# A graph network's attention scores: fp32 products replaced by products of rounded parts and rests

## Chip, core and metric

The kernel runs on one core of a Trainium2 chip. The metric is the device time of one execution in microseconds (us). The engines are PE (TensorE; PEld is its weight load), DVE (VectorE), ACT (ScalarE), POOL (GpSimd) and SP (SyncE, here a queue that issues DMAs). A queue's own DMA issues are shown as SPq, ACTq and POOLq.

## What is computed

Two graph layers over 50,000 nodes and 25,000 edges sorted by destination. The first integrates a graph convolution by four Runge-Kutta steps, the second is an attention layer. Only the attention's first part is touched:

```python
q = (x @ Wq + bq).reshape(n, H, C)          # n nodes, H = 4 heads of C = 32
k = (x @ Wk + bk).reshape(n, H, C)
v = (x @ Wv + bv).reshape(n, H, C)
e = (edge_attr @ We).reshape(-1, H, C)      # edge_attr: 25000 x 32
kj = k[src] + e
vj = v[src] + e
alpha = jnp.einsum('ehc,ehc->eh', q[dst], kj) / np.sqrt(C)
```

Afterwards alpha goes through a softmax per destination and weighs the sum of vj.

## The kernel before

Edges lie in 196 tiles (TE) of 128. The program runs in stages with a barrier between them: `prepare`, `local_pass` (nodes without edges, 0 to about 3250 us of the span with `prepare`), the nine `coupled_stages` (to about 7556 us), and `attention` with `scores`, `shares_beside_far` and `finish_coupled`. This document is about `scores`, lines 1425 to 1569, from about 7563 to 8286 us.

`scores` runs over 98 pairs of edge tiles. Each engine has a list of steps with lags, which `skewed` turns into a loop: at turn t a step of lag n works on pair t - n. Buffers are rings of 4 or 2 slots; `s` is the pair's number modulo 4.

- POOL, `gather` (L1483): four indirect DMAs for each pair, which fetch the rows of x of both tiles' sources and destinations (128 rows of 512 bytes each) into `a_rows`. The pair four back must have been turned. The four issues of all 98 pairs are written out without a loop.
- PE, `turn` (L1502): four 128x128 transposes into one bank. PE, `multiply` (L1510), one pair later: for each of the two tiles, three matmuls that add into one bank of 384 columns (key, value, query): the edges' features with a row of ones against `w_edge` with a row of biases (L1518, 33 rows, 384 wide), the source rows against Wk and Wv (L1520, 256 wide), the destination rows against Wq (L1522, 128 wide). All are fp32, and an fp32 matmul shows as two MATMUL records.
- ACT, `copy` (L1530): the turned rows from PSUM to `a_xt`. ACT, `take` (L1536): value and scaled query out of the banks.
- DVE, `weigh` (L1555): query times key, reduced over each head. DVE, `keep` (L1566), two turns later: 8 columns of alpha.
- SP, `load` (L1464): one DMA of edge features for each pair (33 rows); `store` (L1470) writes the values.

Ahead of the loop SP issues 14 DMAs of weights and biases (`a_weights` 224), for which PE waits.

`local_pass` already works with rounded parts: `product` (L665) adds hi*hi, hi*lo and lo*hi in fp32r, an fp32 whose mantissa the writing engine rounds. There an fp32r matmul shows as one MATMUL record; the profile prints its type as f32. The hi part is written by an ACT copy (L930), the lo part by a DVE subtraction (L985).

Of the kernel before, what the change touches and what calls it, by code (L numbers as in the profile page):

```python
# [1398 lines left out]
def attention(nc, a, S, counts, m):  # L1399

    from contextlib import ExitStack
    ctx = ExitStack()

    def sb(name, shape, dt=F32):
        t = ctx.enter_context(nc.sbuf_tensor(name, list(shape), dt))
        m[name] = t
        return t

    with ctx:
        sb("alpha", [P, TE, HEADS])  # L1410
        sb("w_kvq", [P, 3 * D])
        sb("w_edge", [ED + 1, 3 * D])
        sb("w_skip", [P, D])
        sb("w_up", [P, D])
        sb("w_down", [P, D])
        sb("b_skip", [P, 1])
        sb("b_up", [P, 1])
        sb("b_down", [P, 1])
        sb("neg_half", [P, 2])
        scores(nc, a, S, counts, m)  # L1420
        shares_beside_far(nc, a, S, counts, m)
        finish_coupled(nc, S, counts, m)


def scores(nc, a, S, counts, m):
# [4 lines left out]
    def sb(name, shape, dt=F32):  # L1430
        return ctx.enter_context(nc.sbuf_tensor(name, list(shape), dt))

    pairs = TE // 2
    v, psum, ident = nc.vector, m["psum"], m["ident"]
    ph = counts.phase(pairs, {"gathered*": 64, "own_in*": 16, "turned": 1, "copied": 1,
                              "product": 1, "query": 1, "values": 1, "weighed": 1, "alpha": 1, "stored*": 16})

# [3 lines left out]
    with ctx:  # L1441
        rows = sb("a_rows", [P, 4, 4, D])
        edge = sb("a_edge", [ED + 1, 4, 2 * P])
        xt = sb("a_xt", [P, 2, 4 * P])
        query = sb("a_q", [P, 2, 2, D])
# [3 lines left out]
        with nc.Block() as block:  # L1449
            @block.sync  # L1450
            def _(sp):
                for n, key in enumerate(("Wk", "Wv", "Wq")):
                    sp.dma_start(m["w_kvq"][:, n * D:(n + 1) * D], a["L1_gnn_" + key]).then_inc(S["a_weights"], 16)
                for n in range(2):
                    sp.dma_start(m["w_edge"][0:ED, n * D:(n + 1) * D], a["L1_gnn_We"]).then_inc(S["a_weights"], 16)
                for n, key in enumerate(("bk", "bv", "bq")):
                    sp.dma_start(m["w_edge"][ED:ED + 1, n * D:(n + 1) * D], a["L1_gnn_" + key].unsqueeze(0)
                                 ).then_inc(S["a_weights"], 16)
# [5 lines left out]
                def load(j, s):  # L1464
                    if past(j, 4):
                        sp.wait_ge(S["product"], ph.at("product", j - 4))
                    sp.dma_start(edge[:, s, :], a["edge_attr"][:, bass.ds(j * (2 * P), 2 * P)]
                                 ).then_inc(S[f"own_in{s}"], 16)

# [5 lines left out]
                for s in range(4):  # L1475
                    sp.wait_ge(S[f"stored{s}"], ph.ring_end("stored", s))
                sp.wait_ge(S["a_weights"], 224)

# [19 lines left out]
            def _(pe):  # L1498
                pe.wait_ge(S["a_weights"], 224)
                pe.wait_ge(S["a_zeros"], 1)  # L1500

                def turn(j, s):  # L1502
                    pe.wait_ge(S[f"gathered{s}"], ph.ring_at("gathered", j, s))
                    if past(j, 2):
                        pe.wait_ge(S["copied"], ph.at("copied", j - 2))
                    for i in range(4):
# [3 lines left out]
                def multiply(j, s):  # L1510
                    pe.wait_ge(S["copied"], ph.at("copied", j))
                    pe.wait_ge(S[f"own_in{s}"], ph.ring_at("own_in", j, s))
                    if past(j, 2):
                        pe.wait_ge(S["values"], ph.at("values", j - 2))
                        pe.wait_ge(S["weighed"], ph.at("weighed", j - 2))
                    for i in range(2):
                        bank = psum[2 + 2 * (s % 2) + i]
                        nc.tensor.matmul(bank[:, 0:3 * D], edge[:, s, i * P:(i + 1) * P], m["w_edge"][:],  # L1518
                                         start=True, stop=False)
                        nc.tensor.matmul(bank[:, 0:2 * D], xt[:, s % 2, i * P:(i + 1) * P], m["w_kvq"][:, 0:2 * D],  # L1520
                                         start=False, stop=False)
                        last = nc.tensor.matmul(bank[:, 2 * D:3 * D], xt[:, s % 2, (2 + i) * P:(3 + i) * P],  # L1522
                                                m["w_kvq"][:, 2 * D:3 * D], start=False, stop=True)
                    last.then_inc(S["product"], 1)

                skewed(pe, pairs, [(0, turn), (1, multiply)])

            @block.scalar
            def _(act):
                def copy(j, s):  # L1530
                    act.wait_ge(S["turned"], ph.at("turned", j))
                    if past(j, 2):
                        act.wait_ge(S["product"], ph.at("product", j - 2))
                    nc.scalar.activation(xt[:, s % 2, :], psum[s % 2][:], ACT.Copy).then_inc(S["copied"], 1)

                def take(j, s):  # L1536
# [11 lines left out]
                    last.then_inc(S["query"], 1)  # L1548
                skewed(act, pairs, [(0, copy), (1, take)])

            @block.vector
            def _(dve):
                v.memset(m["w_edge"][0:ED, 2 * D:3 * D], 0.0).then_inc(S["a_zeros"], 1)

# [11 lines left out]
                def keep(j, s):  # L1566
                    dve.wait_ge(S["alpha"], ph.at("alpha", j))
                    v.tensor_copy(m["alpha"][:, bass.ds(j * 2, 2), :], al[:, s, :, :])
                skewed(dve, pairs, [(1, weigh), (3, keep)])

# [685 lines left out]
```

## Time and profile before

| | |
|---|---|
| median of 3 runs | 9125.33 us (9120.25 to 9130.2) |
| profiled execution | 9196.13 us, span 9194.4 us |
| PE busy | 6718.1 us, 73% |
| DVE busy | 6441.7 us, 70% |
| POOL busy | 5499.4 us, 60% |
| ACT busy | 3381.1 us, 37% |
| mean granted clock of PE | 0.862 |

Busy shares are means over very different stages. A stage that ends at a barrier is read by itself: which engine is never idle in it, and how long the others wait for that one. A matmul's duration reaches over its neighbours, since matmuls are pipelined; what one costs is the distance from its start to the next start. The granted clock is a share of 2.4 GHz: 0.50 is 1.2 GHz.

### The profile page before, as it was taken

What the parts mean: (1) busy time and instruction counts of PE and PEld (TensorE: products, weight loads), DVE (VectorE), ACT (ScalarE), POOL (GpSimd) and SP (SyncE); (2) the same over time, 40 slices, a digit from 0 to 9 for tenths busy, and PEclk for the clock granted to TensorE, in tenths of its full rate; (3) what the DMA queues carried; (4) which work ended last, traced back from release to release, by engine and by line L of the source; (5) the groups of instructions that cost most, each with busy time, mean ns of one, the idle gap of its engine ahead of it and who ended that gap; (6) DMA issues with size and microseconds to landing.
All of it is one profiled execution on the core that took longest, in us unless ns stands there. A gap on an engine that the chain in (4) does not pass through costs nothing. (4 is left out here: it accounts for less than half of the span.)

```text
span 9194.4 us, 168134 instructions
## 1 busy us (share of the span) xinstructions
PE 6718.1 (73%) x36044; PEld 5385.6 (59%) x36044; DVE 6441.7 (70%) x17476; ACT 3381.1 (37%) x9316; POOL 5499.4 (60%) x6135
## 2 busy tenths in 40 slices
PE   1600399889988966988897797789666669996665
PEld 0100388888888844766675576667444545554544
DVE  2910388677877888779778977987798981117976
ACT  0000366666666645641361164136100111113323
POOL 0067687777877756755575476557332655545667
PEclk9655799999999977999999999999888985557889
DMA  9333345765444455879879988988898762214544
GB/s 142 86 97 97 100 145 146 123 141 139 143 144 138 139 147 156 249 241 292 250 244 312 315 253 260 335 271 259 280 308 280 210 174 61 60 56 141 169 142 125
DMA packets 1968800, 1693.27 MB, mean 184 GB/s; under 512 B 183280, under 2 KB 1879809, under 8 KB 1968301
## 3 DMA queue, kind: packets, MB, share of 16 engines
q1 hardware_dynamic: 1541549, 1107.88, 42.2%
q0 software_dynamic: 160192, 335.62, 13.1%
q10 hardware_dynamic: 266560, 244.12, 7.8%
q8 instruction: 191, 3.13, 0.2%
q14 instruction: 308, 2.52, 0.1%
HBM read 1063.01 MB, written 624.28 MB: 184 GB/s over the span
## 5 line engine op out<-in xcount | busy, mean ns | idle before, releaser
L1193 PE MATMUL bank<-c_rows,c_sums 128*128 128x256 f32 (+1 forms) x3920 | 1336.0, 425 | 1032.3 <-DVE c_rows L1284 620.7
L680 PE MATMUL bank<-wf_w,c_xt 128*128 128x256 f32 x6272 | 1539.2, 390 | 3.7 <-DVE y L1358 2.6
L1193 PEld LDWEIGHTS bank<-c_rows,c_sums 128*128 128x128 f32 x3920 | 696.7, 203 | 1396.9 <-DVE c_rows L1284 699.3
L1225 ACT ACTIVATE c_xt<-bank 128x512 f32<-128x512 f32 (+1 forms) x980 | 563.5, 575 | 2424.2 <-PE bank L1203 1408.8
L1166 POOL DMA_INDIRECT c_rows<-t_tab,src_row x784 | 872.5, 1113 | 970.7 <-PE bank L1193 807.4
L680 PEld LDWEIGHTS bank<-wf_w,c_xt 128*128 128x128 f32 x6272 | 1231.7, 197 | 185.5 <-issue 3.6
L1284 DVE SCALAR_TENSOR_TENSOR c_rows<-bank,carry,c_rows 32x256 f32<-32x256 f32 (+1 forms) x1950 | 910.6, 467 | 495.6 <-issue 340.5
L1166 POOL DMA_INDIRECT c_rows<-z_tab,src_row x784 | 768.9, 981 | 304.7 <-issue 193.0
L985 DVE TENSOR_TENSOR lx_lo<-bank,lx_hi 128x512 fp32r<-128x512 f32 (+1 forms) x1000 | 658.1, 658 | 350.8 <-ACT lx_hi L930 284.5
L930 ACT ACTIVATE lx_hi<-bank 128x512 fp32r<-128x512 f32 (+1 forms) x1000 | 561.1, 567 | 577.4 <-PE bank L899 457.0
L564 POOL DMA_INDIRECT x_tab<-x_in,stage_pos x396 | 406.3, 1026 | 599.5 <-DMA x_in<-in_x 479.3
L670 PE MATMUL bank<-wf_hi,lx_hi 128*128 128x256 f32 x3200 | 711.2, 304 | 73.5 <-issue 56.4
L1309 DVE SCALAR_TENSOR_TENSOR c_u<-bank,lead,c_own 128x256 f32<-128x256 f32 x1764 | 759.5, 469 | 0.0
L1173 POOL TENSOR_TENSOR c_inv<-c_ss,c_neg_half 128x2 f32<-128x2 f32 x588 | 419.0, 713 | 420.5 <-DVE c_ss L1380 174.0
L670 PE MATMUL bank<-wf_lo,lx_hi 128*128 128x256 f32 x3200 | 643.4, 282 | 0.7 <-issue 0.7
L670 PE MATMUL bank<-wf_hi,lx_lo 128*128 128x256 f32 x3200 | 642.1, 282 | 1.5 <-issue 1.5
L1239 ACT ACTIVATE c_squares<-y,c_root_deg 128x256 f32<-128x256 f32 x980 | 489.9, 500 | 393.5 <-ACT y L1231 238.9
L1203 PE MATMUL bank<-ident,c_u 128*128 128x128 f32 x3724 | 591.5, 281 | 1.0 <-DVE c_u L1309 0.9
L670 PEld LDWEIGHTS bank<-wf_hi,lx_hi 128*128 128x128 f32 x3200 | 494.8, 192 | 106.0 <-issue 84.0
L1203 PEld LDWEIGHTS bank<-ident,c_u 128*128 128x128 f32 x3724 | 487.0, 146 | 97.8 <-issue 6.5
L670 PEld LDWEIGHTS bank<-wf_lo,lx_hi 128*128 128x128 f32 x3200 | 497.3, 191 | 1.4 <-issue 1.4
L670 PEld LDWEIGHTS bank<-wf_hi,lx_lo 128*128 128x128 f32 x3200 | 496.0, 191 | 2.3 <-issue 2.3
(295 smaller groups left out, 15231.3 us busy)
## 6 DMA issues: line engine op xcount, KB each, us to landing
c_z<-z_tab SPq DMA_DIRECT2D x882, 256.0 KB
c_sums<-sum_tab SPq DMA_DIRECT2D x980, 128.0 KB
z_tab<-lz SPq DMA_DIRECT2D x400, 256.0 KB
t_tab<-lt SPq DMA_DIRECT2D x400, 256.0 KB
z_tab<-y ACTq DMA_DIRECT2D x392, 256.0 KB
c_own<-z_tab SPq DMA_DIRECT2D x392, 256.0 KB
t_tab<-y ACTq DMA_DIRECT2D x392, 256.0 KB
c_own<-t_tab SPq DMA_DIRECT2D x392, 256.0 KB
```

Source lines behind the costliest of these rows:

```text
L670: last = nc.tensor.matmul(out, x(k), w[:, k, :], start=(n == 0), stop=(n == 3 * ks - 1 and not bias))
L680: last = nc.tensor.matmul(out, x(k), w[:, k, :], start=(k == 0), stop=(k == ks - 1))
L930: nc.scalar.activation(x_hi[:, k].rearrange("p k n -> p (k n)")[:, 0:n], psum[k][:, 0:n], ACT.Copy).then_inc(S["high"], 1)
L985: v.tensor_tensor(x_lo[:, k].rearrange("p k n -> p (k n)")[:, 0:n], psum[k][:, 0:n], x_hi[:, k].rearrange("p k n -> p (k n)")[:, 0:n].bitc ...
L1166: pool.indirect_dma_start(out=rows[:, s, i, 0:XW] if first else rows[:, s, i, :], out_offset=None, in_=source, in_offset=bass.IndirectOffs ...
L1173: nc.gpsimd.tensor_tensor(inv[:, s, :], ss[:, s, :], m["c_neg_half"][:], ALU.pow).then_inc(S["inverted"], 1)
L1193: nc.tensor.matmul(psum[s % 2][:, i * win:(i + 1) * win], sums[:, s, i, :], rows[:, s, i, 0:win], start=True, stop=True).then_inc(S["summe ...
L1203: last = nc.tensor.transpose(psum[2 + s % 2][:, k * H2 + i * P:k * H2 + (i + 1) * P], u[:, s % 2, i, k * P:(k + 1) * P], ident[:])
L1225: nc.scalar.activation(xt[:, s % 2].rearrange("p k n -> p (k n)")[:, 0:n], psum[2 + s % 2][:, 0:n], ACT.Copy).then_inc(S["copied"], 1)
L1239: last = nc.scalar.activation(m["c_squares"][:, i, :], y[:, s, i, :], ACT.Square, scale=m["c_root_deg"][:, bass.ds(j * 2 + i, 1)], accum_o ...
L1284: v.scalar_tensor_tensor(rows[p0:p0 + 32, s, i, 0:win], before, m["carry"][p0:p0 + 32, bass.ds(j * 2 + i, 1)], rows[p0:p0 + 32, s, i, 0:wi ...
L1309: last = v.scalar_tensor_tensor(u[:, s % 2, i, 0:win], psum[s % 2][:, i * win:(i + 1) * win], m["lead"][:, bass.ds(j * 2 + i, 1)], u[:, s ...
```

## The change

Every fp32 product of `scores` becomes products of fp32r parts. `a_xt` becomes `x_hi` (an ACT copy that rounds) and `x_lo` (a DVE subtraction, new step `low`, from PSUM and `x_hi`). Each of L1520 and L1522 becomes three matmuls: x_hi w_hi, x_hi w_lo, x_lo w_hi. The edges' product becomes one fp32r matmul of 98 rows. The stationary side holds edge features rounded, their rests, and the features rounded again (32 rows each), then two rows of ones; the moving side holds the rounded weights twice, the weights' rests, and the bias' rounded part and rest. For that SP loads the edge features three times (96 rows), ACT rounds all 96 rows (`edge_high`, 96x256), and DVE subtracts in the middle 32 rows (`edge_low`, 32x256). The weights are split once at the start: two ACT copies of 384 columns and four DVE instructions, two of which wait for the one ahead, behind the 18 weight DMAs (`a_weights` 288), with small masks ahead of them. PE waits for all of it (`a_split` 5). `turn` now waits for `low` of two pairs back, `multiply` for `low` and `edge_low` of its pair, `load` for `edge_low` of four pairs back.

The diff, with most of its context left out:

```diff
@@ -1409,7 +1409,6 @@
...
         sb("w_kvq", [P, 3 * D])
-        sb("w_edge", [ED + 1, 3 * D])
         sb("w_skip", [P, D])
...
@@ -1432,16 +1431,30 @@
...
     v, psum, ident = nc.vector, m["psum"], m["ident"]
-    ph = counts.phase(pairs, {"gathered*": 64, "own_in*": 16, "turned": 1, "copied": 1,
-                              "product": 1, "query": 1, "values": 1, "weighed": 1, "alpha": 1, "stored*": 16})
+    ph = counts.phase(pairs, {"gathered*": 64, "own_in*": 48, "turned": 1, "copied": 1,
+                              "product": 1, "query": 1, "values": 1, "weighed": 1, "alpha": 1, "stored*": 16,
+                              "low": 1, "edge_high": 1, "edge_low": 1})
...
         rows = sb("a_rows", [P, 4, 4, D])
-        edge = sb("a_edge", [ED + 1, 4, 2 * P])
-        xt = sb("a_xt", [P, 2, 4 * P])
+        K = 3 * ED + 2
+        edge = sb("a_edge", [3 * ED, 4, 2 * P])
+        edge_parts = sb("a_edge_parts", [K, 4, 2 * P], F32R)
+        w_edge = sb("a_w_edge", [K, 3 * D])
+        w_edge_most = sb("a_w_edge_most", [K, 3 * D])
+        w_edge_hi = sb("a_w_edge_hi", [K, 3 * D], F32R)
+        w_edge_lo = sb("a_w_edge_lo", [K, 3 * D])
+        w_edge_parts = sb("a_w_edge_parts", [K, 3 * D], F32R)
+        w_hi = sb("a_w_hi", [P, 3 * D], F32R)
+        w_lo = sb("a_w_lo", [P, 3 * D], F32R)
+        is_rest = sb("a_is_rest", [P, 1])
+        not_rest = sb("a_not_rest", [P, 1])
+        x_hi = sb("a_x_hi", [P, 2, 4 * P], F32R)
+        x_lo = sb("a_x_lo", [P, 2, 4 * P], F32R)
         query = sb("a_q", [P, 2, 2, D])
...
@@ -1451,10 +1464,13 @@
...
                     sp.dma_start(m["w_kvq"][:, n * D:(n + 1) * D], a["L1_gnn_" + key]).then_inc(S["a_weights"], 16)
+                sp.wait_ge(S["a_zeros"], 1)
                 for n in range(2):
-                    sp.dma_start(m["w_edge"][0:ED, n * D:(n + 1) * D], a["L1_gnn_We"]).then_inc(S["a_weights"], 16)
+                    for part in range(3):
+                        sp.dma_start(w_edge[part * ED:(part + 1) * ED, n * D:(n + 1) * D], a["L1_gnn_We"]
+                                     ).then_inc(S["a_weights"], 16)
                 for n, key in enumerate(("bk", "bv", "bq")):
-                    sp.dma_start(m["w_edge"][ED:ED + 1, n * D:(n + 1) * D], a["L1_gnn_" + key].unsqueeze(0)
+                    sp.dma_start(w_edge[3 * ED:K, n * D:(n + 1) * D], a["L1_gnn_" + key].partition_broadcast(2)
                                  ).then_inc(S["a_weights"], 16)
...
@@ -1463,9 +1479,10 @@
...
                     if past(j, 4):
-                        sp.wait_ge(S["product"], ph.at("product", j - 4))
-                    sp.dma_start(edge[:, s, :], a["edge_attr"][:, bass.ds(j * (2 * P), 2 * P)]
-                                 ).then_inc(S[f"own_in{s}"], 16)
+                        sp.wait_ge(S["edge_low"], ph.at("edge_low", j - 4))
+                    for part in range(3):
+                        sp.dma_start(edge[part * ED:(part + 1) * ED, s, :],
+                                     a["edge_attr"][0:ED, bass.ds(j * (2 * P), 2 * P)]).then_inc(S[f"own_in{s}"], 16)
...
@@ -1474,7 +1491,7 @@
...
                     sp.wait_ge(S[f"stored{s}"], ph.ring_end("stored", s))
-                sp.wait_ge(S["a_weights"], 224)
+                sp.wait_ge(S["a_weights"], 288)
...
@@ -1496,33 +1513,33 @@
...
             def _(pe):
-                pe.wait_ge(S["a_weights"], 224)
-                pe.wait_ge(S["a_zeros"], 1)
+                pe.wait_ge(S["a_split"], 5)
...
                     if past(j, 2):
-                        pe.wait_ge(S["copied"], ph.at("copied", j - 2))
+                        pe.wait_ge(S["low"], ph.at("low", j - 2))
                     for i in range(4):
...
                 def multiply(j, s):
-                    pe.wait_ge(S["copied"], ph.at("copied", j))
-                    pe.wait_ge(S[f"own_in{s}"], ph.ring_at("own_in", j, s))
+                    pe.wait_ge(S["low"], ph.at("low", j))
+                    pe.wait_ge(S["edge_low"], ph.at("edge_low", j))
                     if past(j, 2):
...
                         bank = psum[2 + 2 * (s % 2) + i]
-                        nc.tensor.matmul(bank[:, 0:3 * D], edge[:, s, i * P:(i + 1) * P], m["w_edge"][:],
+                        nc.tensor.matmul(bank[:, 0:3 * D], edge_parts[:, s, i * P:(i + 1) * P], w_edge_parts[:],
                                          start=True, stop=False)
-                        nc.tensor.matmul(bank[:, 0:2 * D], xt[:, s % 2, i * P:(i + 1) * P], m["w_kvq"][:, 0:2 * D],
-                                         start=False, stop=False)
-                        last = nc.tensor.matmul(bank[:, 2 * D:3 * D], xt[:, s % 2, (2 + i) * P:(3 + i) * P],
-                                                m["w_kvq"][:, 2 * D:3 * D], start=False, stop=True)
+                        for x, w in ((x_hi, w_hi), (x_hi, w_lo), (x_lo, w_hi)):
+                            nc.tensor.matmul(bank[:, 0:2 * D], x[:, s % 2, i * P:(i + 1) * P], w[:, 0:2 * D],
+                                             start=False, stop=False)
+                        for n, (x, w) in enumerate(((x_hi, w_hi), (x_hi, w_lo), (x_lo, w_hi))):
+                            last = nc.tensor.matmul(bank[:, 2 * D:3 * D], x[:, s % 2, (2 + i) * P:(3 + i) * P],
+                                                    w[:, 2 * D:3 * D], start=False, stop=(n == 2))
                     last.then_inc(S["product"], 1)
                 skewed(pe, pairs, [(0, turn), (1, multiply)])
...
@@ -1531,7 +1548,13 @@
...
                         act.wait_ge(S["product"], ph.at("product", j - 2))
-                    nc.scalar.activation(xt[:, s % 2, :], psum[s % 2][:], ACT.Copy).then_inc(S["copied"], 1)
+                    nc.scalar.activation(x_hi[:, s % 2, :], psum[s % 2][:], ACT.Copy).then_inc(S["copied"], 1)
+                def edge_high(j, s):
+                    act.wait_ge(S[f"own_in{s}"], ph.ring_at("own_in", j, s))
+                    if past(j, 4):
+                        act.wait_ge(S["product"], ph.at("product", j - 4))
+                    nc.scalar.activation(edge_parts[0:3 * ED, s, :], edge[:, s, :], ACT.Copy).then_inc(S["edge_high"], 1)
...
@@ -1546,11 +1569,44 @@
...
                     last.then_inc(S["query"], 1)
-                skewed(act, pairs, [(0, copy), (1, take)])
+                act.wait_ge(S["a_weights"], 288)
+                nc.scalar.activation(w_hi[:], m["w_kvq"][:], ACT.Copy).then_inc(S["a_high"], 1)
+                nc.scalar.activation(w_edge_hi[:], w_edge[:], ACT.Copy).then_inc(S["a_high"], 1)
+                skewed(act, pairs, [(0, edge_high), (0, copy), (1, take)])
...
             def _(dve):
-                v.memset(m["w_edge"][0:ED, 2 * D:3 * D], 0.0).then_inc(S["a_zeros"], 1)
+                v.memset(w_edge[0:3 * ED, 2 * D:3 * D], 0.0).then_inc(S["a_zeros"], 1)
+                v.tensor_reduce(is_rest[:], ident[:, 2 * ED:3 * ED], AX.X, ALU.add).then_inc(S["a_split"], 1)
+                dve.wait_ge(S["a_split"], 1)
+                v.tensor_tensor(is_rest[:], is_rest[:], ident[:, K - 1:K], ALU.add).then_inc(S["a_split"], 1)
+                dve.wait_ge(S["a_split"], 2)
+                v.tensor_scalar(not_rest[:], is_rest[:], -1.0, 1.0, ALU.mult, ALU.add).then_inc(S["a_split"], 1)
+                for s in range(4):
+                    v.tensor_scalar(edge_parts[3 * ED:K, s, :].rearrange("p (i c) -> p i c", c=P),
+                                    ident[3 * ED:K, :].unsqueeze(1).to_broadcast([2, 2, P]), 0.0, 1.0,
+                                    ALU.mult, ALU.add)
+                dve.wait_ge(S["a_weights"], 288)
+                dve.wait_ge(S["a_high"], 2)
+                dve.wait_ge(S["a_split"], 3)
+                v.tensor_tensor(w_lo[:], m["w_kvq"][:], w_hi[:].bitcast(F32), ALU.subtract)
+                v.tensor_tensor(w_edge_lo[:], w_edge[:], w_edge_hi[:].bitcast(F32), ALU.subtract)
+                v.tensor_scalar(w_edge_most[:], w_edge_hi[:].bitcast(F32), not_rest[0:K, :], None, ALU.mult
+                                ).then_inc(S["a_split"], 1)
+                dve.wait_ge(S["a_split"], 4)
+                v.scalar_tensor_tensor(w_edge_parts[:], w_edge_lo[:], is_rest[0:K, :], w_edge_most[:], ALU.mult, ALU.add
+                                       ).then_inc(S["a_split"], 1)
+                def low(j, s):
+                    dve.wait_ge(S["copied"], ph.at("copied", j))
+                    v.tensor_tensor(x_lo[:, s % 2, :], psum[s % 2][:], x_hi[:, s % 2, :].bitcast(F32), ALU.subtract
+                                    ).then_inc(S["low"], 1)
+                def edge_low(j, s):
+                    dve.wait_ge(S["edge_high"], ph.at("edge_high", j))
+                    mid = edge_parts[ED:2 * ED, s, :]
+                    v.tensor_tensor(mid, edge[ED:2 * ED, s, :], mid.bitcast(F32), ALU.subtract
+                                    ).then_inc(S["edge_low"], 1)
...
@@ -1566,7 +1622,7 @@
...
                     v.tensor_copy(m["alpha"][:, bass.ds(j * 2, 2), :], al[:, s, :, :])
-                skewed(dve, pairs, [(1, weigh), (3, keep)])
+                skewed(dve, pairs, [(0, edge_low), (0, low), (1, weigh), (3, keep)])
...
```

## Rows read from the trace of the kernel before

**Rows 1.** The page: granted clock of TensorE, 40 slices of 230 us.

```profile
PEclk9655799999999977999999999999888985557889
```

**Rows 2.** Busy time of each engine in 100 us of the stage.

```profile
core 0: us, PE busy (x) PEld busy (x) DVE busy (x) ACT busy (x) POOL busy (x), PEclk, DMA share, GB/s
7800.00:7900.00 100.00, 100.00 (x225) 57.27 (x224) 15.11 (x56) 19.17 (x70) 52.65 (x56) 0.50 0.21 59
```

**Rows 3.** Groups of instructions in the stage: count, busy, mean ns, idle before.

```profile
L1518 PE MATMUL bank<-w_edge,a_edge 33*128 33x384 f32 x392 | 322.5, 925 | 7.0 <-issue 4.9 <-DVE a_w L1558 2.1
...
L1490 POOL DMA_INDIRECT a_rows<-x_tab,src_row x196 | 184.8, 943 | 254.5 <-PE bank L1507 215.9 <-issue 33.8 <-remote 4.5
...
L1534 ACT ACTIVATE a_xt<-bank 128x512 f32<-128x512 f32 x98 | 58.7, 599 | 36.4 <-issue 27.0 <-remote 7.6
```

**Rows 4.** Instructions in order of time, one period: start, duration, engine, idle before.

```profile
7905.04 1.06 PE L1507 MATMUL bank<-ident,a_rows 128*128 128x128 f32 x4
...
7906.03 1.65 PE L1518 MATMUL bank<-w_edge,a_edge 33*128 33x384 f32 x2
...
7906.37 0.94 POOL L1490 DMA_INDIRECT a_rows<-x_tab,src_row  x1 [2.48 <-PE bank L1507]
...
7907.60 1.22 PE L1520 MATMUL bank<-w_kvq,a_xt 128*128 128x256 f32 x2
7907.62 0.95 POOL L1490 DMA_INDIRECT a_rows<-x_tab,src_row  x1 [0.30 <-issue]
...
7908.62 0.63 PE L1522 MATMUL bank<-w_kvq,a_xt 128*128 128x128 f32 x2
...
7909.18 1.65 PE L1518 MATMUL bank<-w_edge,a_edge 33*128 33x384 f32 x2
...
7912.20 1.06 PE L1507 MATMUL bank<-ident,a_rows 128*128 128x128 f32 x4
```

**Rows 5.** The same view, the local pass: 256 wide at 1.2 GHz.

```profile
1048.19 0.41 PE L670 MATMUL bank<-w_hi,lx_hi 128*128 128x256 f32 x1
1048.41 0.41 PE L670 MATMUL bank<-w_lo,lx_hi 128*128 128x256 f32 x1
```

**Rows 6.** The same view, the local pass: 128 wide at 1.2 GHz.

```profile
3248.20 0.63 PE L670 MATMUL bank<-w_lo,lx_hi 128*128 128x128 f32 x2
3248.63 0.63 PE L670 MATMUL bank<-w_hi,lx_lo 128*128 128x128 f32 x2
```

**Rows 7.** The same view, the local pass: 256 wide at 2.4 GHz.

```profile
2001.20 0.39 PE L670 MATMUL bank<-wf_hi,lx_lo 128*128 128x256 f32 x2
2001.42 0.39 PE L670 MATMUL bank<-wf_hi,lx_hi 128*128 128x256 f32 x2
```

**Rows 8.** Groups of instructions of the local pass, 1500 to 3000 us.

```profile
L985 DVE TENSOR_TENSOR lx_lo<-bank,lx_hi 128x512 fp32r<-128x512 f32 x609 | 417.1, 685 | 239.3 <-ACT lx_hi L930 184.3 <-issue 53.4
...
L829 POOL DMA_INDIRECT lxo<-x_tab,own_row x135 | 138.8, 1028 | 37.5 <-issue 37.5
...
L1008 DVE TENSOR_TENSOR lrest<-lx_add,b 128x256 f32<-128x256 f32 x68 | 28.6, 420 | 0.0
```

**Rows 9.** Instructions in order of time: start of the stage.

```profile
7564.21 1.02 POOL L1490 DMA_INDIRECT a_rows<-x_tab,src_row  x1 [0.60 <-issue]
...
7568.04 0.94 POOL L1490 DMA_INDIRECT a_rows<-x_tab,dst_row  x1 [0.30 <-issue]
...
7568.98 0.43 SPq L1462 DMA_DIRECT2D b_down<-in_L_gnn_b  x1
...
7571.31 1.11 PE L1507 MATMUL bank<-ident,a_rows 128*128 128x128 f32 x4 [20.82 <-DMA a_rows<-x_tab,dst_row]
```

**Rows 10.** The same view: end of the stage and one copy after it.

```profile
8285.59 0.31 DVE L1568 COPY alpha<-a_al 128x8 f32<-128x8 f32 x3
...
8297.64 0.38 ACT L1831 ACTIVATE fl_xt<-bank 128x256 f32<-128x256 f32 x1
```

**Rows 11.** The gathers of the coupled stages: duration min/median/max in ns.

```profile
L1166 POOL DMA_INDIRECT c_rows<-t_tab,src_row x784: 940/979/1805, 4049.4 to 7067.2; - x196
```

## The prediction

> **What bounds it now.** Read the page's clock line first, then the busy times of the stage, its groups, and one period in order of time. In the page's line the clock falls to about half in slices 33 to 36 [rows 1], which is where `scores` lies. There PE is busy 100 of 100 us at a granted clock of 0.50, that is 1.2 GHz, while DVE is busy 15, ACT 19 and POOL 53 [rows 2]. PE has hardly any idle time ahead of its groups, and POOL's gathers wait 215.9 us in all for PE's transposes [rows 3]. So PE is the bound. One period from transposes to transposes is 7912.20 - 7905.04 = 7.16 us [rows 4]. It holds 7906.03 - 7905.04 = 0.99 of transposes, and for each tile 7909.18 - 7906.03 = 3.15, made of 1.57 for the edges' product, 1.02 for key and value, 0.56 for the query; 0.99 and twice 3.15 are 7.3, less what the last of a pair overlaps. 98 periods are 701 us of the stage, which takes 8285.9 - 7563.5 = 722 us [rows 9, 10].
>
> **PE after.** One MATMUL of rounded parts, 256 wide, costs 1048.41 - 1048.19 = 0.215 us at 1.2 GHz [rows 5]; two of 128 columns cost 3248.63 - 3248.20 = 0.43, so one costs 0.215 as well: half the width brings nothing [rows 6]. At 2.4 GHz two of 256 cost 0.22 [rows 7]. No row shows 384 columns nor 98 rows. The bounds are one 256-wide (0.215) and two (0.43); I take 1.5 times the 256-wide, 0.32, since from 128 to 256 the fixed part already vanished. A tile is then 0.32 + 3 x 0.215 + 3 x 0.215 = 1.61 against 3.15, although it goes from 6 MATMUL records to 7. A pair at 1.2 GHz is 0.99 + 2 x 1.61 = 4.2 us, 4.4 with the upper bound; at 2.4 GHz it is about half. So PE gives back 2.9 us of each 7.16 at the least.
>
> **What is late next.** POOL. Four gathers cost it 4 x (0.943 + 0.30) = 4.97 us [rows 3, 4]; start to start they are 7907.62 - 7906.37 = 1.25. In each period of before it waits 2.48 us for PE [rows 4], and 4.97 + 2.48 - 0.30 = 7.15 closes the period. With PE at 4.2, POOL never waits and the pair costs 4.98. Only 2.18 of PE's 2.9 us reach the end; the other 0.8 becomes PE idle time.
>
> **The added work, each beside that bound of 4.98.**
> - DVE: `low` is the local pass' own instruction at 0.685; `edge_low`, 32 rows by 256, is at most the 128x256 subtraction at 0.42 [rows 8]. With the 15.1 per 100 us of today, 1.08 a pair [rows 2], DVE has 2.2 of 4.98. If that cover were gone it would add up to 1.1 a pair, 108 us.
> - ACT: `edge_high`, 96x256, is near the 128x256 copy at 0.38 [rows 10]; 1.37 of today [rows 2] becomes 1.75. Its wait for features stands ahead of `copy` in ACT's order, so a late load would hold the transposed rows, `low`, and the next `turn`. Loads are issued when `edge_low` of four pairs back is done, some three periods or 15 us ahead.
> - SP: two more issues a pair at 0.43 each [rows 9]; with the first and the store that is 1.7 of 4.98. The wait for `edge_low` now stands ahead of the store of an older pair, which nobody awaits before four more pairs.
> - DMA: 96 rows of 1 KB for 33, while the DMA engines are 21% busy at 59 GB/s [rows 2]; hidden.
> - The hand-over from `turn` to `multiply`: 0.99, copy 0.60 [rows 3], `low` 0.69 and 0.27 for each of two hand-overs (a gather starts at 7906.37 on transposes that end at 7906.10 [rows 4]) make 2.8 us, in which PE multiplies the pair before for 3.2. At 2.4 GHz that is 1.7 us and PE may wait, but a pair is still under 4.98.
> - The start: four more DMA issues of 0.43 move the last weight by 1.7 us, then two ACT copies and four DVE instructions (up to 0.69 each) with hand-overs make 4 to 5. The first transposes, at 7571.3 today [rows 9], come at about 7578. POOL holds four pairs of slots, so it needs them only at 7564.2 + 4 x 4.98 = 7584.1. Price nothing to 6; I take 3, for the first turns of a loop, where the order of time of before has gaps.
>
> **The sum.** First gather at 7564.2 [rows 9]; 98 x 4.98 = 488.0 brings its last issue to 8052.2. A gather lands 7571.31 - 7568.98 = 2.3 later [rows 9]: 8054.5. Then come the last transposes, 0.99, two products of 3.2 (the pair before waits behind them in PE's order), and about 2 for taking (1.37 less the copy's 0.60) and weighing (1.08) [rows 2, 3]: 8063.9. With 3 for the start it is 8067. A gather may also be dearer beside a busier DVE: beside 609 of the same subtraction it took 1.028 with 0.278 between [rows 8], 0.063 more, or 25 us over 392 gathers; DVE is much less loaded here, so I take 8 of nothing to 25. The stage ends at 8075 and not at 8285.9: 211 us less. The other stages aren't touched. The profiled execution of 9196 us would be 8985. It is 71 us (0.8%) above the median of the runs, and no row says where these lie; I carry the difference over whole: 9125.3 - 211 = 8914 us.
>
> **Rivals.**
> 1. Port: `edge_low` reads two operands from SBUF, as no per-pair instruction of the stage does today. If each held up the gather beside it by its whole 0.42, a pair would cost 5.40: 41 us back, 8955. For it: a gather of the coupled stages has taken up to 1.805 against a minimum of 0.940 [rows 11]. Against it: the median there is 0.979. The Trainium skill, page "SBUF — State Buffer", section "Who interferes with whom", says that a DVE instruction with two SBUF inputs contends with a GpSimd instruction that reads SBUF, and that whichever came first holds the port for its whole duration. By it `edge_low` would be the only added per-pair instruction to contend, as `low` has one operand in PSUM. The rows neither confirm it nor exclude it.
> 2. No gain: the steps don't overlap, because a wait of `turn` or `multiply` serialises them. Then a pair is 0.99 + 0.60 + 0.69 + 3.2 + take 0.8 and four hand-overs of 0.27, 7.36 us against 7.16, and the time stays at 9125, 20 more at the most. Against it: two PSUM banks and two slots for each step, as before. A partial chain of 5.5 to 7 us would give 8965 to 9110.
> 3. Slower: gathers at 1.805 [rows 11] plus 0.30 are 8.4 a pair, +124 us, 9249. It decides from 7.16 / 4 = 1.79 us a gather. For it: POOL would run back to back for 490 us with rounding traffic beside it. Against it: even the local pass' mean was 1.31.
> 4. More gain: part of POOL's 0.30 between gathers may be the profiler's own, and PE may rise to 2.4 GHz. At 1.15 a gather, 0.093 less, it is 36 us more, and the tail 3 less: about 8875. No row separates that part; the profiled execution's 71 us above the median are what speaks for it.
>
> **Chances.** Forecast 0.70 (8890 to 8935); port 0.12 (8935 to 8965); more gain 0.07 (8850 to 8890); partial chain 0.04; no gain 0.03; slower 0.04. The range is 8878 to 8962: the forecast, the port and part of the larger gain, about 0.85. A measurement of this kernel can tell about 0.2%, 18 us, from no change. Faster is 0.93, same 0.03, slower 0.04.
>
> **What would show it.** Right: POOL nearly 100% busy or in its 0.30 gaps through the stage, gathers with no wait for PE, a pair every 4.98 us, PE idle some 0.8 us (more if its clock rises) waiting for a gather's landing, and the stage 490 to 515 us long. Three MATMULs 0.215 apart at 1.2 GHz in place of 1.02 show the parts' price; 0.32 from the edges' product to the next shows the 384 columns. Wrong: gathers whose mean is 1.0 or more while `edge_low` runs (rival 1); PE or DVE with waits for each other and POOL still waiting for PE (rival 2); an ACT wait for a load at `edge_high`; or a gap of tens of us before the first transposes.

## Result, and the profile after

| | before | after |
|---|---|---|
| median of 4 runs | 9127.76 us (9120.25 to 9134.89) | 8918.78 us (8910.9 to 8923.26) |
| profiled span | 9194.4 us | 8917.7 us |
| `scores`, first gather to the last copy of alpha | 721.7 us | 505.8 us |

The ratio is 0.977, with a 95% interval of 0.9753 to 0.9787: 209 us less (194 to 225), against a forecast of 211. The profiled spans differ by 277: 216 of it is the stage's, and 60 lies ahead of the stage, in code that the change leaves alone (the first gather of `scores` starts at 7504.3 where [rows 9] have 7564.2). In a later profile of the kernel before with one part of the stage left out (`before_half_gathers`, below) it starts at 7490.2. So the 71 us by which the profiled execution lay above the median came ahead of the stage.

The whole stage after, each engine's busy time beside the granted clock, to be read against [rows 2]:

```profile
core 0: us, PE busy (x) PEld busy (x) DVE busy (x) ACT busy (x) POOL busy (x), PEclk, DMA share, GB/s
7503.00:8010.00 507.00, 372.84 (x1764) 355.90 (x1764) 209.97 (x600) 164.34 (x590) 376.53 (x393) 0.61 0.35 96
```

The groups (count, busy, mean ns, idle before), against [rows 3, 8]; the first two are POOL's four gathers of each pair:

```profile
L1507 POOL DMA_INDIRECT a_rows<-x_tab,dst_row x196 | 191.0, 974 | 59.8 <-issue 59.8
L1507 POOL DMA_INDIRECT a_rows<-x_tab,src_row x196 | 185.5, 946 | 60.0 <-issue 46.3 <-DMA a_rows<-x_tab,dst_row 13.7
L1534 PE MATMUL bank<-a_w_edge_parts,a_edge_parts 98*128 98x384 f32 x196 | 117.7, 600 | 0.6 <-DVE a_x_lo L1602 0.6
L1523 PE MATMUL bank<-ident,a_rows 128*128 128x128 f32 x392 | 97.0, 395 | 144.1 <-DMA a_rows<-x_tab,dst_row 118.1 <-DVE a_w_edge_parts L1597 26.0
...
L1602 DVE TENSOR_TENSOR a_x_lo<-bank,a_x_hi 128x512 fp32r<-128x512 f32 x98 | 67.8, 691 | 51.8 <-ACT a_x_hi L1551 49.8
...
L1557 ACT ACTIVATE a_edge_parts<-a_edge 96x256 fp32r<-96x256 f32 x98 | 41.4, 422 | 0.3 <-DMA a_edge<-in_edge_attr 0.3
...
L1608 DVE TENSOR_TENSOR a_edge_parts<-a_edge,a_edge_parts 32x256 fp32r<-32x256 f32 x98 | 41.1, 419 | 1.4
```

The waits have turned round. POOL waited 215.9 us for PE; now it waits for nobody: its 119.8 us of idle time are the gaps of 0.30 between gathers (the 13.7 put down to a DMA are gaps of the same 0.30 to 0.32), and 376.5 busy plus 119.8 is the stage but for the ends. PE's transposes wait 118.1 us for gathered rows.

In order of time, two stretches of the changed kernel, the first at 2.4 GHz up to its last line, the second, with the last transposes, at 1.2:

```profile
7803.38 0.66 PE L1523 MATMUL bank<-ident,a_rows 128*128 128x128 f32 x4 [1.40 <-DMA a_rows<-x_tab,dst_row]
...
7803.79 0.43 PE L1534 MATMUL bank<-a_w_edge_parts,a_edge_parts 98*128 98x384 f32 x1
...
7804.70 0.39 PE L1534 MATMUL bank<-a_w_edge_parts,a_edge_parts 98*128 98x384 f32 x1
...
7808.74 1.12 PE L1523 MATMUL bank<-ident,a_rows 128*128 128x128 f32 x4 [3.02 <-DMA a_rows<-x_tab,dst_row]
```

```profile
8002.20 1.11 PE L1523 MATMUL bank<-ident,a_rows 128*128 128x128 f32 x4 [1.43 <-DMA a_rows<-x_tab,dst_row]
...
8002.96 0.67 PE L1534 MATMUL bank<-a_w_edge_parts,a_edge_parts 98*128 98x384 f32 x1
...
8003.43 0.41 PE L1537 MATMUL bank<-a_w_hi,a_x_hi 128*128 128x256 f32 x1
8003.64 0.41 PE L1537 MATMUL bank<-a_w_lo,a_x_hi 128*128 128x256 f32 x1
...
8004.60 0.63 PE L1534 MATMUL bank<-a_w_edge_parts,a_edge_parts 98*128 98x384 f32 x1
```

At 1.2 GHz a tile takes 8004.60 - 8002.96 = 1.64 us and a pair 0.76 + 2 x 1.64 = 4.04; at 2.4 GHz a tile takes 0.91. Either way PE is done before the next rows land. The clock moves between the levels, 0.61 of full on average.

### The profile page after: what moved, and what is told of

It is laid out like the page before. It is cut to its first block and busy times, and to the rows that moved or that the text cites. A ratio compares the mean times of both kernels' runs of the same rounds, so it can differ in the third digit from the quotient of the medians.

```text
span 8917.7 us, 169344 instructions
## 1 busy us (share of the span) xinstructions
PE 6364.0 (71%) x36240; PEld 5328.2 (60%) x36240; DVE 6550.1 (73%) x17683; ACT 3419.5 (38%) x9416; POOL 5489.1 (62%) x6135
## 3 DMA queue, kind: packets, MB, share of 16 engines
q8 instruction: 192, 3.15, 0.2%
## 5 line engine op out<-in xcount | busy, mean ns | idle before, releaser
L564 POOL DMA_INDIRECT x_tab<-x_in,stage_pos x396 | 379.7, 959 | 609.5 <-DMA x_in<-in_x 489.1
```

## Experiments

The kernels ran in three groups, each on one chip with runs of the kernel before beside it. First group, 9112.4 us for the kernel before: `before_half_gathers`, `after_half_gathers`, `edges_only`, `nodes_only`. Second, 9108.8: `fp32_128_rows`, `half_gathers_33_rows`, `edge_rest_wide`, `psum_extra`. Third, 9109.9: `fp32_128_again`, `after_again`, `fp32_128_rows_half_gathers`, `no_edge_rest`. By the ratio 0.977 the changed kernel lies at about 8903 on the first; in the third it was measured. The 8919 in the first expectations is from another chip, some 15 us slower.

### What bounds each stage: half of the gathers

In both kernels, the same edit (the count of landings that is waited for is halved too):

```diff
-                    for n, which in enumerate((m["src_row"], m["dst_row"])):
+                    for n, which in enumerate((m["src_row"],)):
...
-                        last = nc.tensor.transpose(psum[s % 2][:, i * P:(i + 1) * P], rows[:, s, i, :], ident[:])
+                        last = nc.tensor.transpose(psum[s % 2][:, i * P:(i + 1) * P], rows[:, s, i % 2, :], ident[:])
```

> The kernel before with two of its four gathers for each pair; the destinations' rows are left out and the sources' rows turned in their place, so the queries are of the wrong nodes. Theory (PE bounds the stage of before at 7.16 us a pair, POOL waits 2.5 of them): the time stays at 9128 within 15 us, POOL's wait grows to about 5 us a pair. Rival (the gathers or their landing bound it): 2.5 us a pair less, 245 us, 8880.

Measured 9102.99 us, ratio 0.9992 (0.9982 to 1.0002): no change. POOL's gathers in order of time:

```profile
7800.24 0.94 POOL L1490 DMA_INDIRECT a_rows<-x_tab,src_row  x1 [4.97 <-PE bank L1507]
7801.49 0.94 POOL L1490 DMA_INDIRECT a_rows<-x_tab,src_row  x1 [0.31 <-issue]
7807.40 0.94 POOL L1490 DMA_INDIRECT a_rows<-x_tab,src_row  x1 [4.97 <-PE bank L1507]
```

The period is still 7.16, and the freed 2.49 us became a wait for PE (4.97 for 2.48 in [rows 4]). PE bound the stage of before.

> The changed kernel with two of its four gathers for each pair, in the same way. Theory (POOL's gathers bound the changed stage at 5.05 us a pair): a pair falls to PE's own time, which the trace of the changed kernel gives as 0.77 + 2 x 1.64 = 4.05 us at 1.2 GHz and 0.41 + 2 x 0.87 = 2.15 at 2.4 GHz, or to VectorE's chain at about 2.7 if the clock rises: between 98 and 230 us less than 8919, so 8690 to 8821. Rival (PE or a chain of hand-overs bounds it at 5.05, and the gathers only happen to fit): it stays at 8919 within 15 us.

Measured 8675.17 us, ratio 0.9521 (0.9505 to 0.9537), some 228 us under the changed kernel and at the low end of what I expected (8690, which is some 15 less on this chip). So POOL bounds the changed stage, and what comes next is far below: a pair takes 2.68 us ((7755.05 - 7495.44) / 97 between the first and the last transposes), at the full clock. 100 us of it, columns as above, and the group with PE's idle time:

```profile
7600.00:7700.00 100.00, 84.27 (x670) 80.40 (x669) 78.21 (x223) 57.66 (x225) 70.35 (x75) 1.00 0.50 134
```

```profile
L1534 PE MATMUL bank<-a_w_edge_parts,a_edge_parts 98*128 98x384 f32 x196 | 80.0, 408 | 37.4 <-DVE a_x_lo L1602 36.3 <-ACT a_v L1564 0.4
```

No engine is full there; PE at 84 and DVE at 78 are near it, and PE's waits inside the loop are for DVE's `a_x_lo` (36.3 us). So the hand-over from the transposes over copy and `low` to the products is a candidate for what sets the 2.68; no run tests it.

### One half of the change at a time

`edges_only` has the stacked edges' product and whole fp32 rows for the nodes:

```diff
-        x_hi = sb("a_x_hi", [P, 2, 4 * P], F32R)
+        x_hi = sb("a_x_hi", [P, 2, 4 * P])
...
-                        for x, w in ((x_hi, w_hi), (x_hi, w_lo), (x_lo, w_hi)):
-                            nc.tensor.matmul(bank[:, 0:2 * D], x[:, s % 2, i * P:(i + 1) * P], w[:, 0:2 * D],
-                                             start=False, stop=False)
+                        nc.tensor.matmul(bank[:, 0:2 * D], x_hi[:, s % 2, i * P:(i + 1) * P], m["w_kvq"][:, 0:2 * D],
+                                         start=False, stop=False)
...
```

> Only the edges' product is in rounded parts (98 rows); the nodes' products are fp32 of the whole rows as before, and DVE writes one column in place of the nodes' rests. Theory: PE at 1.2 GHz needs 0.9 + 2 x (0.43 + 1.02 + 0.56) = 4.9 us a pair, about what POOL's gathers need, so nearly the whole gain is here: a pair at 5.05 to 5.2, 8919 to 8940 us. Rival (the gain needs both halves of the change in proportion to PE's time, 2.3 of 3.1 us a pair): 9128 - 0.74 x 209 = 8973.

`nodes_only` keeps the 33 fp32 rows for the edges, with their loads and waits as before, and splits the nodes' rows as the change does:

```diff
-                        nc.tensor.matmul(bank[:, 0:3 * D], edge_parts[:, s, i * P:(i + 1) * P], w_edge_parts[:],
+                        nc.tensor.matmul(bank[:, 0:3 * D], edge33[:, s, i * P:(i + 1) * P], w33[:],
                                          start=True, stop=False)
```

> Only the nodes' products are in rounded parts; the edges' product is one fp32 matmul of 33 rows as before. Theory: PE stays the bound at 0.9 + 2 x (1.57 + 1.2) = 6.4 us a pair at 1.2 GHz, 0.7 less than before: 9128 - 72 = about 9055, between 9040 and 9070. Rival 1 (the clock rises with the rounded products, since the activity of narrow fp32 ones is what kept it low): PE falls under POOL and the time is near 8920 to 8950. Rival 2 (as with both halves): 8919.

Measured: `edges_only` 8899.23 us, ratio 0.9766 (0.9749 to 0.9782), the whole gain. `nodes_only` 9088.23 us, ratio 0.9975 (0.9965 to 0.9985): 24 us, a third of what I expected. The windows of the two, `edges_only` first:

```profile
7600.00:7900.00 300.00, 187.82 (x840) 162.13 (x840) 89.28 (x360) 99.18 (x356) 227.06 (x240) 0.81 0.36 98
```

```profile
7600.00:7900.00 300.00, 300.00 (x865) 188.10 (x863) 69.26 (x215) 59.41 (x215) 162.46 (x173) 0.50 0.22 61
```

The time of `edges_only` came out as I had it, but PE's part in it did not. I had PE at 1.2 GHz for 4.9 us a pair, just under the gathers. The trace has the clock at 0.81 and PE idle 112 of 300 us. Where it is at 1.2 GHz, one tile of `edges_only` reads:

```profile
7801.38 0.67 PE L1534 MATMUL bank<-a_w_edge_parts,a_edge_parts 98*128 98x384 f32 x1
7801.85 1.05 PE L1536 MATMUL bank<-w_kvq,a_x_hi 128*128 128x256 f32 x2
7802.69 0.63 PE L1538 MATMUL bank<-w_kvq,a_x_hi 128*128 128x128 f32 x2
...
7802.98 0.67 PE L1534 MATMUL bank<-a_w_edge_parts,a_edge_parts 98*128 98x384 f32 x1
```

That is 1.60 us a tile and, with 0.75 of transposes, 3.95 a pair, against 1.64 and 4.04 in the changed kernel at the same clock. The nodes' fp32 products take 0.84 + 0.29 there, their rounded parts 0.64 + 0.53. So the nodes' parts save PE nothing, and `edges_only` is under the gathers at either clock.

`nodes_only` stays at 0.50 with PE never idle, and its order of time shows a price that I had left out:

```profile
7802.76 1.65 PE L1533 MATMUL bank<-a_w,a_edge 33*128 33x384 f32 x2
...
7804.33 0.58 PE L1536 MATMUL bank<-a_w_hi,a_x_hi 128*128 128x256 f32 x1
...
7804.71 0.41 PE L1536 MATMUL bank<-a_w_lo,a_x_hi 128*128 128x256 f32 x1
7804.92 0.41 PE L1536 MATMUL bank<-a_w_hi,a_x_lo 128*128 128x256 f32 x1
```

The first product of 128 rows after one of 33 costs 0.38 us, the next ones 0.21. So I asked whether the 33 rows by themselves, and not the fp32 passes, made the stage slow.

### The rows of the edges' product alone

`fp32_128_rows` is the kernel before with the narrow product padded by zeros. Nothing is rounded, split or loaded beyond what it was:

```diff
-        sb("w_edge", [ED + 1, 3 * D])
+        sb("w_edge", [P, 3 * D])
...
-        edge = sb("a_edge", [ED + 1, 4, 2 * P])
+        edge = sb("a_edge", [P, 4, 2 * P])
...
+                sp.wait_ge(S["a_zeros"], 1)
...
-                    sp.dma_start(edge[:, s, :], a["edge_attr"][:, bass.ds(j * (2 * P), 2 * P)]
+                    sp.dma_start(edge[0:ED + 1, s, :], a["edge_attr"][:, bass.ds(j * (2 * P), 2 * P)]
...
-                v.memset(m["w_edge"][0:ED, 2 * D:3 * D], 0.0).then_inc(S["a_zeros"], 1)
+                v.memset(edge[:], 0.0)
+                v.memset(m["w_edge"][:], 0.0).then_inc(S["a_zeros"], 1)
```

> The kernel before with one thing changed: the tiles of the edges' product have 128 rows in place of 33, of which 95 hold zeros that DVE writes once at the start. The products stay fp32, their number and widths too. Theory (the clock: the narrow product is what holds PE at 1.2 GHz in this stage): the clock rises, PE needs 0.45 + 2 x (0.79 + 0.51 + 0.28) = 3.6 us a pair and the gathers become the bound as in the changed kernel: 0.977 of before, about 8905. Rival (the cheaper passes of the rounded parts brought the gain): clock and time stay as before, 9112.

Measured 8894.5 us, ratio 0.9766 (0.9749 to 0.9782). The same 300 us and one tile of it:

```profile
7600.00:7900.00 300.00, 199.06 (x963) 148.41 (x961) 59.67 (x240) 82.77 (x300) 226.89 (x241) 0.99 0.31 86
```

```profile
7702.44 0.81 PE L1519 MATMUL bank<-w_edge,a_edge 128*128 128x384 f32 x2
...
7703.09 0.59 PE L1521 MATMUL bank<-w_kvq,a_xt 128*128 128x256 f32 x2
...
7703.52 0.38 PE L1523 MATMUL bank<-w_kvq,a_xt 128*128 128x128 f32 x2
7703.74 0.81 PE L1519 MATMUL bank<-w_edge,a_edge 128*128 128x384 f32 x2
```

The same fp32 products that took 3.15 us a tile in [rows 4] take 1.30. The granted clock went from 0.50 to 0.99, the 2.4 GHz level, by the rows alone. PE had been busy without a gap at 0.50, so idle time was not what held it there. The first products of this run still show the 1.2 GHz level:

```profile
7498.05 1.48 PE L1519 MATMUL bank<-w_edge,a_edge 128*128 128x384 f32 x2
...
7500.61 1.48 PE L1519 MATMUL bank<-w_edge,a_edge 128*128 128x384 f32 x2
```

A tile takes 2.56 us there, 0.59 less than with 33 rows. With 0.9 of transposes that is an estimate of 6.0 us a pair at 1.2 GHz, still above the gathers' 5.0, where the 2.4 GHz level gives 3.04 (below). So of the 7.16 the evened rows take 1.1 and the clock 3.0, and without the clock padding would have brought about half of the gain.

The counterpart takes rows from the rounded product, with half of the gathers so that PE can be the bound:

```diff
-                        nc.tensor.matmul(bank[:, 0:3 * D], edge_parts[:, s, i * P:(i + 1) * P], w_edge_parts[:],
+                        nc.tensor.matmul(bank[:, 0:3 * D], edge_parts[0:ED + 1, s, i * P:(i + 1) * P], w_edge_parts[0:ED + 1, :],
```

> The changed kernel with half of the gathers, and the edges' product over the first 33 of its 98 rows (the edges' rests, the weights' rests and the biases are left out; the destinations' rows too). PE's instructions are the same in number and width. Theory (a product of few rows holds the clock low also in rounded parts): PE at 4.05 us a pair, 8675 + 98 x 1.37 = 8809. Rival (only fp32 products of few rows do): the clock rises and the time is that of the half gathers with 98 rows, 8675.

Measured 8905.22 us, ratio 0.9777 (0.9761 to 0.9794): 230 us above the half gathers with 98 rows, and 96 above my figure. The clock came out as expected, the price of a pair did not:

```profile
7600.00:7900.00 300.00, 300.00 (x1072) 234.04 (x1072) 131.13 (x358) 91.72 (x354) 112.45 (x120) 0.50 0.27 72
```

```profile
7699.88 0.69 PE L1534 MATMUL bank<-a_w_edge_parts,a_edge_parts 33*128 33x384 f32 x1
...
7700.50 0.58 PE L1537 MATMUL bank<-a_w_hi,a_x_hi 128*128 128x256 f32 x1
...
7700.88 0.41 PE L1537 MATMUL bank<-a_w_lo,a_x_hi 128*128 128x256 f32 x1
...
7701.62 0.41 PE L1540 MATMUL bank<-a_w_hi,a_x_lo 128*128 128x128 f32 x1
...
7701.97 0.69 PE L1534 MATMUL bank<-a_w_edge_parts,a_edge_parts 33*128 33x384 f32 x1
```

A tile takes 2.09 us where 98 rows take 1.64 at the same clock: 0.62 for 0.47 on the narrow product, 0.38 for 0.21 on the one behind it, 0.35 for 0.21 on the last one before the next narrow. Over a pair the two tiles and the transposes between (1.00 for 0.76) add up to 1.0: 5.05 for 4.04, from 7699.88 to the next pair's 7704.93.

This run also answers whether rounding by itself frees PE. With 33 rows and the clock at 0.50 throughout, all products rounded, PE needs 5.05 us a pair where the kernel before needs 7.16, about what four gathers cost. The narrow product alone fell from 1.57 to 0.62 a tile.

### What the rounded parts bring by themselves

> The kernel before with the edges' product padded to 128 rows of fp32, once more, beside the changed kernel on one chip. Theory (POOL's gathers bound both stages, PE at 3.1 or 4.05 us a pair is under them): the two differ by what DVE's rounding costs the gathers, 7 us, and by a few us at the start: this one 5 to 12 us under the changed kernel. Rival (the rounded parts bring something of their own): the changed kernel is ahead by more than 10 us.

> The changed kernel as it is, beside the padded fp32 one. Theory: 0.977 of before, 5 to 12 us above the padded one.

On one chip, five rounds: padded fp32 8894.88 us, ratio 0.9763 (0.975 to 0.9776); changed kernel 8905.63, ratio 0.9774 (0.9761 to 0.9788). The difference of 10.8 us is the expected size, but the intervals overlap and the profiles give the stage only 3.6 of it (499.2 us for 502.8); there the first gather starts at 7486.9 and 7498.0, so most of the rest lies ahead of the stage. The padded fp32 kernel is at least as fast, without new loads and with less DVE and ACT work.

`fp32_128_rows_half_gathers` joins the edits of the half gathers and of the padding:

> The padded fp32 kernel with half of the gathers (the destinations' rows are left out). What the rounded parts would be worth if the gathers were not the bound. Theory: PE bound at 2.4 GHz, 0.49 + 2 x 1.30 = 3.1 us a pair against 2.68 of the changed kernel with half of the gathers: 8675 + 98 x 0.42 = 8716. Rival (a busier PE loses the clock again): 4.5 us or more a pair, above 8850.

Measured 8702.13 us, ratio 0.9554 (0.9539 to 0.9569), 14 under my figure. A pair takes 3.04:

```profile
7600.00:7700.00 100.00, 100.00 (x529) 79.23 (x528) 32.40 (x132) 42.07 (x165) 62.14 (x66) 1.00 0.35 97
```

PE is busy without a gap at 1.00, as it was in the kernel before at 0.50: with rows of 128 a full PE keeps the upper level. With the rounded parts it was 8675.17, on another chip. So the parts save 27 us by the times, 31 by the stages (278.9 us for 310.0), but only where the gathers are no longer the bound.

### The port between DVE and POOL

> The changed kernel with three more subtractions of the size of the edges' rest (32 x 256) in each pair, both operands in SBUF, results unused. Theory of cover and port: DVE has room for 1.25 us more in 5.05, and a gather that starts in the first 0.3 us of such an instruction is held until it has read; four times as many such starts, so the gathers' mean grows by four times the 0.016 us of now: 20 to 25 us more than the changed kernel. Rival 1 (DVE's time on the path): 98 x 1.25 = 122 us more. Rival 2 (no port): nothing.

```diff
                 def edge_low(j, s):
                     dve.wait_ge(S["edge_high"], ph.at("edge_high", j))
                     mid = edge_parts[ED:2 * ED, s, :]
+                    for k in range(3):
+                        v.tensor_tensor(spare[ED:2 * ED, 3 * s + k, :], edge[ED:2 * ED, s, :], edge[ED:2 * ED, s, :], ALU.subtract)
```

> The changed kernel with three more subtractions of the same size in each pair, but one operand in PSUM. Theory of the port: DVE's time grows as in the run before, yet no gather is held by them: the changed kernel's time within 10 us, gathers of 0.943 except those beside the edges' rest. Rival (any busier DVE makes gathers dearer): as the run before.

```diff
+                    for k in range(3):
+                        v.tensor_tensor(spare[ED:2 * ED, 3 * s + k, :], psum[s % 2][ED:2 * ED, 0:2 * P],
+                                        x_hi[ED:2 * ED, s % 2, 0:2 * P].bitcast(F32), ALU.subtract)
```

> The changed kernel with DVE's subtraction of the edges' rest left out (DVE writes one column of zeros in its place), so no instruction of each pair reads two operands from SBUF. Theory of the port: no gather is longer than 1.0 us where 26 of 372 were over 1.05, the mean of the destinations' gathers falls from 0.974 to 0.944, the stage is 6 to 8 us shorter. Rival (any DVE work does it): the long gathers stay.

```diff
-                    v.tensor_tensor(mid, edge[ED:2 * ED, s, :], mid.bitcast(F32), ALU.subtract
-                                    ).then_inc(S["edge_low"], 1)
+                    v.memset(mid[:, 0:1].bitcast(F32), 0.0).then_inc(S["edge_low"], 1)
```

Measured: `edge_rest_wide` 8907.67 us (0.9761 to 0.9793 of before), `psum_extra` 8902.09 (0.9756 to 0.9788), `no_edge_rest` 8897.84 in a single run. The times alone can't separate these. What they do show is the cover: 1.2 us more of DVE a pair is nowhere near the 122 us that it would be on the path. The gathers' groups separate the rest; `edge_rest_wide`, `psum_extra` and `no_edge_rest` in this order:

```profile
L1508 POOL DMA_INDIRECT a_rows<-x_tab,dst_row x196 | 194.7, 994 | 59.8 <-issue 59.8
L1508 POOL DMA_INDIRECT a_rows<-x_tab,src_row x196 | 186.7, 953 | 60.1 <-issue 55.2 <-DMA a_rows<-x_tab,dst_row 4.9
```

```profile
L1508 POOL DMA_INDIRECT a_rows<-x_tab,dst_row x196 | 189.1, 965 | 59.8 <-issue 59.8
```

```profile
L1507 POOL DMA_INDIRECT a_rows<-x_tab,src_row x196 | 185.4, 946 | 60.0 <-issue 45.7 <-DMA a_rows<-x_tab,dst_row 14.3
L1507 POOL DMA_INDIRECT a_rows<-x_tab,dst_row x196 | 185.0, 944 | 59.8 <-issue 59.8
```

Without the subtraction no gather between 7530 and 7980 us is over 0.97 us, and the stage takes 499.6 us, where the two profiles of the changed kernel have 505.8 and 502.8. With it, in the changed kernel, 26 of some 370 gathers between 7520 and 7990 are over 1.05, and each of the 26 started while the subtraction ran, as this one did:

```profile
7799.40 0.41 DVE L1608 TENSOR_TENSOR a_edge_parts<-a_edge,a_edge_parts 32x256 fp32r<-32x256 f32 x1
7799.44 1.19 POOL L1507 DMA_INDIRECT a_rows<-x_tab,dst_row  x1 [0.31 <-issue]
```

A gather that starts 0.05 us after the subtraction does takes 1.19, one at 0.15 takes 1.09, one at 0.23 takes 1.00, and from 0.29 on it takes 0.94: it is held until 0.29 us into the subtraction. One that starts up to 0.04 us behind it isn't held (0.94). With an operand in PSUM nothing is held: the 73 gathers that started beside the added subtractions of `psum_extra` took 0.95 at most. But three more subtractions made the gathers only 5.3 us dearer in all (994 for 974 and 953 for 946, 196 times each), not the 20 to 25 that I expected: the gathers that started beside such a subtraction went from 59 of 355 to 95 of 352, and not to four times as many. So the mechanism is shown and its size was put too high.

## Why the prediction was right, and where its reasons were not

- **The bound of before**, PE at 7.16 us a pair with 2.48 of wait on POOL: shown, by taking two gathers away for nothing.
- **PE after**, 4.2 us a pair at 1.2 GHz: 4.04 measured where the clock is at that level. The edges' product took 0.47 and not 0.32, above even the upper bound of 0.43, but the first of the three 128-wide products took 0.11 and not 0.215, so the tile's 1.61 came out at 1.64: two errors that cancel.
- **What is late next**, POOL at 4.98: 5.0 in most periods (the median is 5.01), and it decided the time. That step carries the 211 us. Rivals 2 and 3 fell with it: the second needed a chain of waits, and POOL waits for nobody; the third needed 1.79 us a gather, and the longest took 1.22 without its gap.
- **Dearer gathers**, 8 us: 31 and 3 ns on 196 gathers each are 6.7. Rival 1 had the right mechanism at six times its price. The Trainium skill, page "SBUF — State Buffer", section "Who interferes with whom", says that the shared port is an exclusive lock, and its section "SBUF: two separate sides" that whoever starts first gets it for the whole instruction; here the hold ended at 0.29 us of the 0.41 that the trace gives the subtraction. That two operands in SBUF are what holds it agrees with the runs.
- **The start**, 3 us: the first transposes came 12.3 us after the first gather, 13.8 expected, and POOL never waited for them. The term should have been nothing. The end was 2 us shorter as well, so the stage took 505.8 us where the sum has 511. By the profiles it gained 216, by the medians 209, and both are within the interval: that the time came within 2 us of the forecast is partly luck.
- **The profiled 71 us**, carried over whole: right. Rival 4's larger gain, a gap between gathers that is partly the profiler's, fell: the profiled execution of the changed kernel took 8919.5 us, the others 8910.9 to 8923.3.
- **The reason for PE's relief held, but only for the smaller half of the edit.** The prediction priced PE at either level of the clock and found both under POOL, so its time didn't depend on the clock, and the rounded parts do free PE at 1.2 GHz: 7.16 us a pair falls to 5.05 with 33 rows and to 4.04 with 98. But it took each product's parts to pay. Nearly all of it came from the edges' product: one MATMUL record for two of fp32, 1.57 to 0.62 us a tile, and then 1.0 a pair because it is no longer so much narrower in rows than its neighbours. The nodes' parts, by far the larger half of the edit, are worth 24 us alone, and nothing beside the stacked edges.
- **A second way to the same time was not seen.** Zeros in 95 rows, with nothing rounded, bring the whole gain, about half of it by the rows' own price and the rest by the clock (0.50 to 0.99). So rounding is sufficient here and not necessary.
- The trace of before held a clue: PE busy 100 of 100 us at 0.50, while the coupled stages with fp32 products of 128 rows stood at 7 to 9 tenths, mostly 9 [rows 1]. I read the clock as given and did not ask what differed.

What stays open is how many rows are needed for the upper level of the clock.

## What to carry to other kernels

When PE is busy without a gap and its granted clock is still 1.2 GHz, look at the rows of its products before their type: padding the narrow one to 128 rows with zeros gave here what a rewrite into rounded parts gave. Before splitting a product into parts, price it beside neighbours of the same rows: the nodes' fp32 products looked dear (1.58 us a tile) mostly because of the narrow one next to them (1.13 without it). Before costing a faster engine, price the next one in the same period: of the 3.1 us a pair that PE gave back at the least, POOL's gathers let 2.2 through. And move one half of a double change at a time; here all of the gain was in the smaller half.

## What the runs showed of the hardware that I had not expected

- Product rows and clock: with 33 rows in one of three products, 0.50 with PE busy throughout; with 128 rows of which 95 are zero, 0.99, and 1.00 with PE busy throughout (`fp32_128_rows_half_gathers`); with 98 rows, 0.61 in the changed kernel, where PE waits for each pair's rows, 0.81 in `edges_only`, and 1.00 in the half gathers, with PE busy 84 of 100 us.
- At 1.2 GHz in rounded parts, a product of 128 rows behind one of 33 costs 0.38 us for 0.21, the narrow one 0.62 where one of 98 rows costs 0.47, and the one ahead of it 0.35 for 0.21. In fp32 a tile costs 3.15 with 33 rows and 2.56 with 128.
- Of the three rounded products of 128 columns behind those of 256, the first costs 0.11 us at 1.2 GHz and the next two 0.21 each, as much as one of 256.
- A gather on POOL that starts 0.05 to 0.28 us into a DVE subtraction with both operands in SBUF is held until 0.29 us into it, which makes it up to 1.19 us long for 0.94 in the changed kernel; with one operand in PSUM it is not held.
